# Deformable sampling: x weights as one ramp on second differences of the values, late images' points read from the banks

## The reference, cut to what matters

```python
value = (t @ Wv + bv).reshape(N, H, W, G, Cg)               # G = 4 groups of 8 channels
om = (t @ Wom + bom).reshape(N, H, W, G, 3 * K)             # K = 9 points
loc_y = ys + ky + offset[..., 1]
loc_x = xs + kx + offset[..., 0]
sampled = _bilinear_gather(value, loc_y, loc_x)             # outside the image: zero
out = (sampled * mask[..., None]).sum(axis=4)
return out.reshape(N, L, C) @ Wo
```

## Time and profile before

| | |
|---|---|
| median of 3 runs | 417.6 us (416.93 to 417.88) |
| the profiled execution | 417.61 us, span 415.7 us |
| mean granted clock of PE | 0.988 |
| samples of the first turn | 155.32 to 228.4 us of the span |
| samples of the second turn | 242.91 to 316.1 us |

### The profile page before, as it was taken

The page is one execution under the profiler, slowest core; times in us unless marked ns, Lnnn a source line. Parts: engine busy times, 40 slices in busy tenths (PEclk is TensorE's granted clock), DMA queues, the critical chain, the costliest instruction groups (busy, mean ns, idle before and its releaser), DMA issues.

```text
span 415.7 us, 9843 instructions
## 1 busy us (share of the span) xinstructions
PE 379.2 (91%) x3994; PEld 260.5 (63%) x3994; DVE 331.9 (80%) x656; ACT 289.8 (70%) x516; POOL 165.5 (40%) x140
## 2 busy tenths in 40 slices
PE   6789999989899898899999998989999999999897
PEld 5576942223236766676777665667678787666575
DVE  3859797998974478899999588999997686999451
ACT  4846296998946479997770599987822627999471
POOL 5002200000000049889998278999994050000000
PEclk9988999999999999999999999999999989999999
DMA  8300040000007000000000000000000000000000
GB/s 297 143 2 0 2 97 2 2 0 2 2 0 278 0 2 2 2 3 2 1 2 2 2 2 2 2 2 2 2 2 1 2 2 1 2 2 1 2 2 27
DMA packets 1629, 9.29 MB, mean 22 GB/s; under 512 B 208, under 2 KB 976, under 8 KB 1104
## 3 DMA queue, kind: packets, MB, share of 16 engines
q1 hardware_dynamic: 1440, 8.59, 5.8%
q10 hardware_dynamic: 144, 0.07, 0.1%
HBM read 7.40 MB, written 0.26 MB: 18 GB/s over the span
## 4 chain that ended last, share of the span: by engine, by line
PE 34%; DVE 32%; ACT 16%; POOL 8%; issue 8%; DMA 1%; DVEq 0%; SPq 0%; ACTq 0%
PE bank L1398 6%; PE bank L1128 4%; DVE PRD L985 4%; DVE wb L985 4%; POOL PRD L374 3%; PE bank L1478 3%; ACT RINGS L599 3%; ACT RINGS L669 2%; DVE RINGS L883 2%; ACT RINGS L602 2%; DVE RINGS L874 2%; POOL wb L374 2%; PE bank L1387 2%; DVE SMT L997 2%; PE bank L1274 2%
## 5 line engine op out<-in xcount | busy, mean ns | idle before, releaser
L1478 PE MATMUL bank<-VB,RINGS 64*128 64x144 f32 x1152 | 93.0, 298 | 5.9 <-DVE PRD L985 3.0
L1478 PEld LDWEIGHTS bank<-VB,RINGS 64*128 64x128 f32 x1152 | 75.6, 186 | 27.7 <-issue 10.1
L1128 PE MATMUL bank<-cst 128*128 128x128 f32 x422 | 59.4, 284 | 0.0
L357 POOL TENSOR_TENSOR HY<-OM,cst 128x324 f32<-128x324 f32 x16 | 11.5, 748 | 116.8 <-DVE LXA L930 113.0
L1128 PEld LDWEIGHTS bank<-cst 128*128 128x128 f32 x422 | 53.1, 195 | 5.2 <-issue 2.8
L985 DVE TENSOR_TENSOR wb<-bank,HY 128x864 f32<-128x864 f32 x48 | 50.3, 1049 | 4.6 <-PE bank L1478 4.5
L985 DVE TENSOR_TENSOR PRD<-bank,HY 128x864 f32<-128x864 f32 x48 | 50.0, 1049 | 4.0 <-PE bank L1478 4.0
L599 ACT ACTIVATE RINGS<-bank,cst 128x768 f32<-128x768 f32 x48 | 42.4, 883 | 15.3 <-PE bank L1461 15.1
L602 ACT ACTIVATE RINGS<-RINGS,cst 128x768 f32<-128x768 f32 x48 | 44.9, 936 | 1.6
L540 ACT ACTIVATE RINGS<-PRD,wb 128x2048 f32<-128x2048 f32 (+1 forms) x21 | 39.5, 1921 | 4.5 <-PE bank L1398 3.4
L1398 PE MATMUL bank<-RINGS,cst 128*32 128x512 f32 x336 | 39.7, 594 | 2.4 <-DVE RINGS L883 2.0
(11 more groups left out here) (277 smaller groups left out, 704.0 us busy)
## 6 DMA issues: line engine op xcount, KB each, us to landing
wd<-in_wd SPq DMA_DIRECT2D x1, 2793.0 KB, 9.6
wb<-in_wb SPq DMA_DIRECT2D x1, 2112.0 KB, 10.2
wc<-in_wc SPq DMA_DIRECT2D x1, 1027.0 KB, 12.2
cst<-in_cst SPq DMA_DIRECT2D x1, 766.0 KB, 5.1
PRD<-PRD SPq DMA_DIRECT2D x1, 324.0 KB, 3.7
PRD<-PRD SPq DMA_DIRECT2D x1, 323.9 KB, 5.0
PRD<-PRD SPq DMA_DIRECT2D x1, 323.8 KB, 4.4
XC<-in_x SPq DMA_DIRECT2D x2, 128.0 KB, 2.4
```

The lines of the kernel that those rows point to most:

```text
L1128: pe.matmul(bk[:, 0:P], ident, ident, start=True, stop=True)
L1478: ins = pe.matmul(view(bank[q % 2 * 2 + gp], k3 * NR, [[3 * NR, 2 * CG], [1, NR]]), view(HX, b % 2 * HXN + (3 * t + k3) * NPIX + half * P, ...
```

## The change

The tent in x is replaced by a single ramp. A piecewise linear function of x that is zero on the left of the image is a sum of ramps, weighted by the second differences of its values; so the values are computed from second differences of the source along x, and the x weight of a column is max(0, 16 - k - u) with u = max(0, 15 - x), the latter in the copy of the turned points. Right of the image's last column the sum would not fall off, and a factor min(1, max(0, 16 - x)) goes into the mask. The constants `mx`, `last` and `past` are now 16 - k, 15 and 16.

- ACT: `hats` has one pass in place of two. The source is copied to a padded XP; `points_out` gets the max; the copies of the masks go, and `right_edge` makes max(0, 16 - x) for each of three groups of points (image 0, images 1 to 3, images 4 to 7).
- POOL: `second_differences` for each of the source's two halves: first differences XD, then second ones in XW; it stands before `rows_off(0)` and behind it. `masked(0)` is now ahead of `rows_off(1)` to `(3)`. Once, before the first turn, XP is cleared and the values' bias BV made.
- PE: the late images' offsets go to banks 3 and 7, on top of the base (`based_last`, two matmuls of 432 columns), ahead of the turning of image 0's points; that turning uses bank 6. New waits on `mm_ready`: the first spread for group 0's masks, product 0 for group 1's, the turning of image 1 and product 1 for group 2's.
- DVE: `points` reads all three groups from the banks (the late one with its two compares split by half); `offsets` and the points from SBUF go. `modulation` multiplies min(1, edge) by the mask, into MM; the third stands behind sample 0.

```diff
+POINTS = ((0, 1, bank[4], 3 * KG), (1, B4 - 1, bank[0], 512), (B4, B4, (bank[3], VALS), 4 * 512))
+def pieces_of(group):
+    return ((0, 1), (1, 1)) if group == 2 else ((0, 2),)
...
-        pool.wait_ge(lxa_ready, pointed(turn, b if b < 2 else B4))
+        pool.wait_ge(lxa_ready, pointed(turn, b))
...
     def masked(turn, b):
         pool.wait_ge(hy_ready, B * turn + b + 1)
+        pool.wait_ge(mm_ready, pointed(turn, b))
         for half in range(2):
             hy = by_trio(HY, (2 * b + half) * HYN)
             ins = pool.tensor_tensor(hy, hy, by_point(MM, 2 * b + half), ALU.mult)
         ins.then_inc(hym_ready, 1)
+    def second_differences(turn, bh):
+        n = NBH * turn + bh + 1
+        xp, xd = bh * HH * XPW, bh * HH * (XPW - 1)
+        pool.wait_ge(xp_ready, n)
+        shifted = lambda s: view(XP, xp + s, [[XPW, HH], [1, XPW - 1]])
+        pool.tensor_tensor(view(XD, xd, [[XPW - 1, HH], [1, XPW - 1]]), shifted(1), shifted(0), ALU.subtract).then_inc(xd_ready, 1)
+        pool.wait_ge(xd_ready, n)
+        after(pool, val_done, VALUE_PIECES * turn)
+        shifted = lambda s: view(XD, xd + s, [[XPW - 1, NR], [7 * (XPW - 1), NA], [1, WW]])
+        pool.tensor_tensor(view(XW, bh * NR * NA * WW, [[NA * WW, NR], [WW, NA], [1, WW]]), shifted(1), shifted(0),
+                           ALU.subtract).then_inc(xw_ready, 1)
...
+    pool.wait_ge(wc_s, 16)
+    pool.wait_ge(lo_ready, NBH)
+    pool.memset(view(XP, 0, [[1, NBH * HH * XPW]]), 0.0).then_inc(xp_clear, 1)
+    pool.tensor_tensor(view(BV, 0, [[1, VALS]]), view(wc, WC["bval"], [[1, VALS]]), view(cst, CST["edge"], [[0, VALS]]),
+                       ALU.mult).then_inc(bv_ready, 1)
     for turn in range(2):
+        second_differences(turn, 0)
         rows_off(turn, 0)
+        second_differences(turn, 1)
+        masked(turn, 0)
         rows_off(turn, 1)
-        masked(turn, 0)
         rows_off(turn, 2)
         rows_off(turn, 3)
...
         act.wait_ge(t_done, i + 1)
         after(act, sel_done, 9 * (i - 1))
-        act.activation(view(LXT, i % 2 * NPIX, [[1, NPIX]], n=LXW), bank[7][0:LXW, 0:NPIX],
-                       ACT.Copy).then_inc(lxt_ready, 1)
+        act.activation(view(LXT, i % 2 * NPIX, [[1, NPIX]], n=LXW), bank[7 if i % B else 6][0:LXW, 0:NPIX], ACT.Relu,
+                       scale=-1.0, bias=cst[0:LXW, CST["last"]:CST["last"] + 1]).then_inc(lxt_ready, 1)
+    def right_edge(turn, group):
+        b, count, bk, half_step = POINTS[group]
+        act.wait_ge(lxa_ready, 3 * turn + group + 1)
+        for half, halves in pieces_of(group):
+            ins = act.activation(view(LX, (2 * b + half) * KG, [[KG, halves], [2 * KG, count], [1, KG]]),
+                                 view(bk, half * half_step, [[half_step, halves], [3 * KG, count], [1, KG]]), ACT.Relu, scale=-1.0,
+                                 bias=cv("past", 1))
+        ins.then_inc(edge_ready, 1)
...
         hx = i % 2 * HXN + 3 * t * NPIX
         act.wait_ge(sel_done, 9 * i + 3 * t + 3)
-        act.activation(view(HX, hx, [[NPIX, 3], [1, NPIX]]), view(bank[4], 0, [[512, 3], [1, NPIX]]), ACT.Abs,
-                       bias=cv("mx", 1)).then_inc(abs_done, 1)
-        act.wait_ge(abs_done, 3 * i + t + 1)
-        act.activation(view(HX, hx, [[1, 3 * NPIX]]), view(HX, hx, [[1, 3 * NPIX]]), ACT.Relu, scale=-1.0,
-                       bias=cv("one", 1)).then_inc(hat_ready, 1)
+        act.activation(view(HX, hx, [[NPIX, 3], [1, NPIX]]), view(bank[4], 0, [[512, 3], [1, NPIX]]), ACT.Relu, scale=-1.0,
+                       bias=cv("mx", 1)).then_inc(hat_ready, 1)
     def deform(turn, src, src_ready, counts):
-        after(act, val_done, VALUE_PIECES * turn)
+        act.wait_ge(xp_clear, 1)
+        after(act, xd_ready, NBH * turn)
         for bh in range(NBH):
             act.wait_ge(src_ready, counts[bh])
-            act.activation(view(XW, bh * NR * NA * WW, [[NA * WW, NR], [WW, NA], [1, WW]]),
-                           view(src, bh * NPIX, [[WW, NR], [7 * WW, NA], [1, WW]]), ACT.Copy).then_inc(xw_ready, 1)
-        act.wait_ge(lxa_ready, pointed(turn, 0))
-        act.activation(view(MM, 0, [[KG, 2], [1, KG]]), view(bank[4], 2 * KG, [[3 * KG, 2], [1, KG]]),
-                       ACT.Copy).then_inc(mm_ready, 1)
+            act.activation(view(XP, bh * HH * XPW + 2, [[XPW, HH], [1, WW]]), view(src, bh * NPIX, [[WW, HH], [1, WW]]),
+                           ACT.Copy).then_inc(xp_ready, 1)
+        right_edge(turn, 0)
         for b in range(B):
             i = B * turn + b
             if b == 0:
                 points_out(i)
-                act.wait_ge(lxa_ready, pointed(turn, 1))
-                act.activation(view(MM, 2 * KG, [[KG, 2], [2 * KG, B4 - 1], [1, KG]]),
-                               view(bank[0], 2 * KG, [[512, 2], [3 * KG, B4 - 1], [1, KG]]), ACT.Copy).then_inc(mm_ready, 1)
+                right_edge(turn, 1)
                 rows_hat(i)
             for t in range(3):
                 hats(i, t)
+                if b == 0 and t == 0:
+                    right_edge(turn, 2)
...
-    def first_points(turn, bk, half_step, b, count):
-        dve.wait_ge(om_done, 6 * turn + (2 if b == 0 else 4))
-        am = view(AM, 2 * b * KG, [[KG, 2], [2 * KG, count], [1, KG]])
-        ly = view(bk, KG, [[half_step, 2], [3 * KG, count], [1, KG]])
+    def points(turn, group):
+        b, count, bk, half_step = POINTS[group]
+        dve.wait_ge(om_done, 2 * (3 * turn + group + 1))
+        def beyond(test):
+            for half, halves in pieces_of(group):
+                ins = dve.tensor_scalar(view(AM, (2 * b + half) * KG, [[KG, halves], [2 * KG, count], [1, KG]]),
+                                        view(bk, half * half_step + KG, [[half_step, halves], [3 * KG, count], [1, KG]]),
+                                        8.0, -FAR, test, ALU.mult)
+            link(ins)
         def columns_of(a):
...
                                         view(bk, half * half_step, [[3 * KG, count], [12, 3], [1, 12]]), ALU.add)
             return ins
-        link(dve.tensor_scalar(am, ly, 8.0, FAR, ALU.is_ge, ALU.mult))
+        beyond(ALU.is_ge)
         columns_of(0)
...
-        link(dve.tensor_scalar(am, ly, 8.0, FAR, ALU.is_lt, ALU.mult))
+        beyond(ALU.is_lt)
         columns_of(1).then_inc(lxa_ready, 1)
-    def offsets(turn, half):
-        dve.wait_ge(om_done, 6 * turn + 5 + half)
-        dve.tensor_tensor(view(OM, (2 * B4 + half) * KG, [[2 * B * KG, 3], [2 * KG, B4], [1, KG]]),
-                          view(bank[half], 0, [[KG, 3], [3 * KG, B4], [1, KG]]),
-                          view(base, half * 3 * KG, [[KG, 3], [0, B4], [1, KG]]), ALU.add).then_inc(om_used, 1)
-        dve.wait_ge(om_used, 2 * turn + half + 1)
-    def points(b, count):
...
-        link(dve.tensor_scalar(flat(AM), flat(LY), 8.0, None, ALU.is_ge))
-        dve.scalar_tensor_tensor(lxa[0], twelves(AM), BIG, twelves(LX), ALU.mult, ALU.add)
-        link(dve.scalar_tensor_tensor(flat(LY), flat(AM), -7.0, flat(LY), ALU.mult, ALU.add))
-        link(dve.tensor_scalar(flat(AM), flat(AM), -1.0, 1.0, ALU.mult, ALU.add))
-        dve.scalar_tensor_tensor(lxa[1], twelves(AM), BIG, twelves(LX), ALU.mult, ALU.add).then_inc(lxa_ready, 1)
+    def modulation(turn, group):
+        b, count, bk, half_step = POINTS[group]
+        dve.wait_ge(edge_ready, 3 * turn + group + 1)
+        for half in range(2):
+            at = (2 * b + half) * KG
+            ins = dve.scalar_tensor_tensor(view(MM, at, [[2 * KG, count], [1, KG]]), view(LX, at, [[2 * KG, count], [1, KG]]), 1.0,
+                                           view(bk, half * half_step + 2 * KG, [[3 * KG, count], [1, KG]]), ALU.min, ALU.mult)
+        ins.then_inc(mm_ready, 1)
...
     def values(turn):
+        dve.wait_ge(bv_ready, 1)
...
-        first_points(turn, bank[4], 3 * KG, 0, 1)
-        first_points(turn, bank[0], 512, 1, B4 - 1)
+        points(turn, 0)
+        points(turn, 1)
+        modulation(turn, 0)
+        modulation(turn, 1)
         values(turn)
-        offsets(turn, 0)
-        offsets(turn, 1)
-        points(B4, B4)
+        points(turn, 2)
         for b in range(B):
             i = B * turn + b
             for u in range(IMQ):
                 sample(i, *divmod(u, 2))
+                if b == 0 and u == 0:
+                    modulation(turn, 2)
...
+    def based_last():
+        for half in range(2):
+            pe.matmul(bank[3 + 4 * half][:, VALS:VALS + 12 * KG], ident, view(base, half * 3 * KG, [[0, 4], [1, 3 * KG]]), start=True, stop=False,
+                      skip_group_check=True)
...
+        if b == 1:
+            pe.wait_ge(mm_ready, 3 * turn + 3)
         for half in range(2):
-            ins = pe.transpose(bank[7][0:LXW, half * P:(half + 1) * P], view(LXA, (b * 2 + half) * LXW, [[1, LXW]]), ident)
+            ins = pe.transpose(bank[7 if b else 6][0:LXW, half * P:(half + 1) * P], view(LXA, (b * 2 + half) * LXW, [[1, LXW]]), ident)
...
```

(24 more changed lines are left out.)

32 lines of the change are left out of this document (17 added, 15 removed).

## The result

The changed kernel takes **424.8 us** (median of 4 runs, 423.68 to 425.45), the kernel before 417.5 (4 runs, 416.93 to 417.88). The ratio is 1.0172, with a 95% interval of 1.0154 to 1.0189: 7.3 us slower, where the forecast was 1.3 us slower, and outside its range of 416.6 to 421.4. The profiled execution took 425.45 us, its span is 423.7, so it stands 7.84 us over the profiled one of before (417.61). Its mean granted clock is 0.972; the other three runs, of which there is no trace, have 0.980 to 0.984.

A forecast was written before the change was run, and what follows sets the result against it. No single bound: DVE limits images 4 to 7, ACT image 1, PE the stretch from product 1 to image 1. +2.5, -1.9 and 0.05 make +0.65 us a turn, +1.3 in two: 418.9 us, range 416.6 to 421.4.

The forecast's parts named there:

- The path to image 1: Start of each turn: later turning and values, then product 1 waiting for the late modulation; image 1 begins 2.5 us later.
- DVE's path to sample 0: Turn start on DVE: values' end, modulation 0 and 1, then late points, ending at 155.65, within 0.1 of the other path.
- PE's clock falls: Rival, chance 0.20: PE's idle gaps around the start of the samples lower the granted clock; 420.1 or 421.3 us.
- the forecast's own: PE's predicted idle gap of 1.6 us around the start of the samples, between 153.4 and 157.25.
- The rival: PE's clock falls, chance 0.20: 3.4 us at the lower level lose 1.2 us, all in the stretch that PE bounds.
- the rival's 421.3: Time in us if PE's clock falls in both turns; 420.1 with one turn hit.
- Image 1: Image 1 of each turn: one x pass fewer on ACT shortens it to 8.65 us, -1.9 us a turn.
- my bound of 9.1: Upper bound for image 1 in us: the length of image 2, the nearest with PE's extra work.
- my walk of the ring: Image 1's estimate through two pairs of banks, where product q waits for sample q-2; it gave 8.65 us.
- POOL: POOL's subtractions at the turn's start and sooner row distances of images 1 to 3 are hidden and cost nothing.
- The sum: +2.5 for image 1's later start, -1.9 for image 1, 0.05 for image 2: +0.65 us a turn, two turns +1.3.
- 0 to +1.6 a turn: Bounds of the sum: image 1 between 8.33 and 9.1 us, product 1 between 157.2 and 158.1.

The follow-up runs named there:

- e1: The changed kernel with six keep-warm matmuls on PE behind product 0 of each turn; 420.72 us.
- e11: The kernel before with one wait more: PE turns image 1's points only when sample 0 of the turn is done; 423.54 us.
- e2: The changed kernel with the third modulation ahead of sample 0 instead of behind it; 419.0 us.
- e3: The changed kernel with late points through SBUF as in the kernel before, and image 0's points turned ahead of all values; 420.65 us.
- e8: e1 with one entry of PE's table moved, spread 4 behind product 4 in place of 5; 420.0 us.
- e6: e3 with POOL's row subtractions no sooner than in the kernel before; 415.57 us.
- e10: e6 with spread 4 behind product 4 in PE's table, as in e8; 414.96 us.
- e5: The kernel before with the changed kernel's late points alone, offsets read from banks 3 and 7; 420.26 us.

## Why the prediction was wrong

- **The path to image 1, but for the clock: right.** Turning 150.6 (150.23), values' end 152.2 (about 151.7), sample 0 155.7 (155.64), turning of image 1 157.25 (157.27), product 1 157.6 (157.84). The wait that I named, `modulation` 2 behind sample 0, is the one that the trace names. One detail was off without effect: DVE's path to sample 0 ended 0.47 us ahead of PE's, where I had put the two within 0.1. With the clock at its higher level image 0 lasts 9.84 and 9.90 us (e1), and with the 0.5 at the start image 1 begins 2.5 us later than before, as forecast.
- **The failed step: the clock.** I gave "PE's clock falls" a chance of 0.20 and left it out of the sum, because in the kernel before the clock stayed at 1.00 "through PE's stalls behind ACT as well". Those stalls are under 0.7 us each at that place, the forecast's own was 1.6; my argument compared unlike gaps, while the only rows that I showed with PE idle for as much of the time were the rival's. e1 (fill the gap, 4.1 us back) and e11 (make the gap in the kernel before, 6.0 us lost, of which some 3.6 are the two waits themselves) show it from both sides. With the gap filled the time is 420.7, inside my range. That a like gap does not always bring the fall, as in e2 and e3, is shown too, so a chance was the right form for it; its weight and its price were wrong.
- **The clock's price: too low.** The rival had 3.4 us at half clock, 1.2 us a turn. It lasted 6.8 us in each turn and cost 2.8 and 2.9. So even the rival's 421.3 missed. Each of the three low stretches inside the trace of before, at 20.2, 33.8 and 334.2, lasts 3.4 us, and I took their length for a constant.
- **Image 1: mis-sized.** Forecast 8.65, measured 9.10 and 9.21, near my bound of 9.1. The chain of spread and pass at 1.83 us a round, three spreads in a row by the table, was not in my walk of the ring; e8 moves one spread and gets 8.59, with 0.3 more in image 0. That is 0.5 us a turn. Image 2 took 9.35 in place of about 9.15: 0.2 a turn. It comes with the ramp, for it is 9.35 in every kernel that has it, e6 and e10 too, and 9.10 in e5 and e11; by what step was not tried.
- **The two halves.** Of the 2.5 us by which image 1 begins later, 1.5 come with the late offsets from banks alone (e5, where sample 0 is 0.6 us later and image 0 0.9 longer); the other 1.0 goes by subtraction to the `modulation` wait, which has no run of its own.
- **POOL: right for the changed kernel, not in general.** The two subtractions and the sooner rows cost nothing that its trace shows. In e3 the same sooner rows stretched DVE's late points by 1.7 us a turn (3.8 from 154.20 to 157.96, against 2.0 from 153.99 to 156.01 in e6). There DVE reads SBUF alone; in the changed kernel the same points come from banks, and a pair of instructions takes 0.51 to 0.52, the first pair (152.57), when POOL stands still, like the four behind it, when POOL is at work.
- **The sum.** +0.5 for the start and +2.0 for image 0 with its clock, +2.8 for the clock, -1.4 for image 1, +0.3 for image 2: some +4.2 a turn, against the forecast's +0.65. The forecast was not quite consistent in its bounds either: 0 to +1.6 a turn is 417.6 to 420.8, where it says 418.4 to 420.6.

## What to carry to other kernels

Before a change that puts one wait of a microsecond or more on TensorE between short bursts, price the granted clock as well as the wait, and do not take the length of the low stretch from another place: it was 3.4 us there and 6.8 here. Like waits did and did not bring the fall within one trace, so several runs are needed to see it. A few filling matmuls behind the last product before the wait are a cheap test. An engine's saved pass is worth what the shared bank or ring lets it be: look for two engines that hand the same buffers back and forth several times in a row. And of a change in several parts run the parts: here the ramp with neither rearrangement (e6) gained 2 us, with the rows made sooner (e3) it lost 3, and with the late offsets from the banks as well, as the change was made, it lost 7.

## What the runs showed of the hardware

- The granted clock fell to 0.50 with no single gap on PE longer than 1.75 us in the changed kernel and 1.03 in e2, behind stretches with PE busy for 1.64 of 3.40 us, and stayed there for 6.8 us although PE was busy through nearly all of it (6.80 of 6.80 in e11). It did not fall each time: in the first turn of e2 and in the second of e3 it stayed at 1.00 behind the same gaps and the same busy time (1.64 and 1.65 of 3.40) as in the turn where it fell.
- Two-input VectorE instructions out of SBUF (128x288) took 0.89 to 1.00 us beside GpSimd's subtractions and 0.45 to 0.46 without, and a `TENSOR_SCALAR` 0.74 against 0.31. GpSimd's x6 took 5.14 us there, against 4.27 in the changed kernel, where VectorE was reading banks. The samples (128x864, one operand from a bank) stayed at 1.06 either way. The Trainium skill, SBUF — State Buffer, section "SBUF: two separate sides", says that VectorE and GpSimd share one pair of ports, held for a whole instruction and needed by a VectorE instruction only when it has two SBUF inputs or runs in a two-port mode: the rows agree as to which instructions are slowed and which are not. That 0.89 is 0.46 and a wait for GpSimd's instruction in hand is then likely, but the rows do not show a wait apart.
